# A graph attention with 8192 nodes: who clears the gather buffer, and behind which block each attention stands

## The reference

```python
feats   = (x @ W).reshape(N, H, D)
a_self  = einsum('nhd,hd->nh', feats, att_self)
a_neigh = einsum('nhd,hd->nh', feats, att_neigh)
scores  = leaky_relu(a_self.T[:, :, None] + a_neigh.T[:, None, :], 0.2)
scores  = scores - 1e10 * (1 - adj)
out     = einsum('hij,jhd->ihd', softmax(scores), feats) + bias
y       = layernorm(x + relu(out))
```

## Time and profile before

| | us |
|---|---|
| median of 3 runs (lowest, highest) | 844.21 (843.2, 846.03) |
| the profiled execution, its own time | 844.56 |
| its span, first to last instruction | 842.7 |
| TensorE busy with matmuls (share) | 600.1 (71%) |
| VectorE busy | 587.8 (70%) |
| GpSimd busy | 502.0 (60%) |
| ScalarE busy | 78.2 (9%) |
| moved by transfers | 291.79 MB |

### The profile page before, as it was taken

How to read it: one execution, slowest core, us unless ns; L and a number is a source line. 1 busy time by engine, 2 the same in 40 slices (tenths; PEclk the granted TensorE clock), 3 DMA queues, 4 the chain that set the end, 5 groups by cost and what they waited for, 6 DMA issues and landing times.

```text
span 842.7 us, 8722 instructions
## 1 busy us (share of the span) xinstructions
PE 600.1 (71%) x2132; PEld 289.6 (34%) x2133; DVE 587.8 (70%) x1683; ACT 78.2 (9%) x355; POOL 502.0 (60%) x464
## 2 busy tenths in 40 slices
PE   2766665588669797868888786976769685835564
PEld 1621111146314352433424251533335141504343
DVE  5567994641796878676666675677668977847885
ACT  1200000210010101000001000011020110102010
POOL 4100977777607777777777777766464757636400
PEclk9885555558979988886868695989799696958787
DMA  7999999999999999999999999999999999931100
GB/s 284 363 413 389 408 391 345 329 359 398 399 419 404 398 399 397 401 396 399 398 399 399 398 398 398 397 400 396 373 369 408 399 406 397 403 136 27 37 1 25
DMA packets 76230, 291.79 MB, mean 346 GB/s; under 512 B 31318, under 2 KB 39307, under 8 KB 43408
## 3 DMA queue, kind: packets, MB, share of 16 engines
q1 hardware_dynamic: 56784, 275.44, 83.4%
q0 software_dynamic: 14208, 10.46, 4.3%
q10 hardware_dynamic: 5184, 5.31, 1.9%
HBM read 294.39 MB, written 4.75 MB: 355 GB/s over the span
## 4 chain that ended last, share of the span: by engine, by line
DMA 52%; PE 27%; DVE 13%; issue 5%; SPq 1%; ACT 1%; DVEq 0%; ACTq 0%
DMA adj_sb<-in_adj_dram 51%; PE xt_ps L676 13%; PE codes L648 11%; DVE spare L926 2%; DVE head_mask L792 1%; PE ft_ps L633 1%; PE xt_ps L678 1%; PE ft_ps L717 1%; SPq L402 1%; DVE top L912 1%; DMA base<-in_L_gnn_att_self_dram 1%; DVE z L903 1%; DVE z L911 1%; DVE z L915 0%; DVE z L906 0%
## 5 line engine op out<-in xcount | busy, mean ns | idle before, releaser
L444 POOL DMA_INDIRECT near<-node_table,idx x444 | 489.6, 1103 | 278.6 <-issue 192.9
L648 PE MATMUL codes<-adj_sb,weights 128*128 128x512 bf16 x1024 | 349.5, 482 | 165.1 <-DMA adj_sb<-in_adj_dram 164.8
L648 PEld LDWEIGHTS codes<-adj_sb,weights 128*128 128x128 bf16 x1024 | 100.6, 109 | 393.7 <-issue 339.2
L676 PE MATMUL xt_ps<-spare,ident 128*128 128x360 f32 (+4 forms) x734 | 195.4, 416 | 29.6 <-DVE spare L926 29.6
L676 PEld LDWEIGHTS xt_ps<-spare,ident 128*128 128x128 f32 x734 | 135.5, 198 | 81.5 <-issue 41.8
L816 DVE MAX8 val<-codes 128x8 f32<-128x128 f32 x192 | 42.7, 284 | 140.7 <-PE codes L648 134.0
L926 DVE TENSOR_TENSOR spare<-near,spare 128x704 f32<-128x704 f32 (+12 forms) x64 | 101.1, 1641 | 9.1 <-ACT spare L571 9.1
L821 DVE MAX8 val<-codes 128x8 f32<-128x64 f32 (+2 forms) x156 | 19.6, 198 | 42.8 <-PE codes L648 42.0
L571 ACT ACTIVATE spare<-z 128x736 f32<-128x736 f32 (+10 forms) x16 | 14.9, 933 | 215.4 <-DVEq L918 215.4
L641 PE MATMUL codes<-place,weights 128*128 128x512 bf16 x64 | 31.3, 490 | 0.0
L872 DVE MAX8 key<-left 128x8 f32<-128x168 f32 (+2 forms) x79 | 28.7, 363 | 2.7
(11 more groups left out here) (156 smaller groups left out, 483.6 us busy)
## 6 DMA issues: line engine op xcount, KB each, us to landing
adj_sb<-in_adj_dram SPq DMA_DIRECT2D x256, 1024.0 KB, 16.7
near<-node_table,idx POOLq DMA_INDIRECT x444, 5.8
node_table<-spare ACTq DMA_DIRECT2D x4, 648.0 KB, 7.9
spare<-in_x_dram SPq DMA_DIRECT2D x4, 512.0 KB, 7.7
self_sb<-node_table ACTq DMA_DIRECT2D x16, 121.5 KB, 7.6
x_sb<-in_x_dram SPq DMA_DIRECT2D x4, 384.0 KB, 18.1
out_dram<-x_sb SPq DMA_DIRECT2D x1, 768.0 KB, 12.6
self_sb<-node_table ACTq DMA_DIRECT2D x16, 40.5 KB, 10.1
```

What stands on the lines that cost most here:

```text
L444: pool.indirect_dma_start(out=near[:, near_at(t) + k, :], out_offset=None, in_=table[:, :], in_offset=bass.IndirectOffsetOnAxis(ap=idx[t % ...
L648: last = pe.matmul(codes[i][:, :], weights[:, kk, :], adj_bf[q][:, k * GC:(k + 1) * GC, 1], start=False, stop=(kk == BITS - 1))
L676: last = pe.matmul(to[:, a:b, :], ident[:, :], slot_rows(t, s, a, b), start=(s == 0), stop=(s == W - 1))
```

## The change

Two edits. First, the clearing of `near` goes from POOL, where it stood behind `weights_ready`, to VectorE, as its first instruction; POOL still waits for it (`near_zeroed`) ahead of its first gather. Second, `ATTEND` is changed from turn 6 on: the turns 6 to 10 come three blocks apart, then after a space of four again three. With it the sums and finishes move. Behind the last packing stand two attentions (turns 14 and 15, at 64 and 67), and the sums of turns 13 to 15; turn 12's sums stand in block 62. Turns 6, 10 and 11 now stand behind the last block of a turn (39, 51 and 55), where before it was turn 8 (47).

```diff
-    ATTEND = [16, 20, 24, 28, 32, 36, 40, 44, 47, 50, 53, 57, 60, 64, 67, 70]
+    ATTEND = [16, 20, 24, 28, 32, 36, 39, 42, 45, 48, 51, 55, 58, 61, 64, 67]
...
-            pool.wait_ge(weights_ready, 1)
-            pool.memset(near[:, :, :], 0.0).then_inc(near_zeroed, 1)
 
             pool.wait_ge(table_written, 16 * XG)
             pool.wait_ge(near_zeroed, 1)
...
+            dve.memset(near[:, :, :], 0.0).then_inc(near_zeroed, 1)
             dve.wait_ge(params_loaded, 64)
 
             step(dve.memset(wa, 0.0))
```

## The result

The changed kernel takes 830.39 us (median of 4 runs, 829.19 to 831.54) against 844.8 us for the kernel before (median of 4, run beside it): a ratio of 0.9834, 95% interval 0.9812 to 0.9856. The forecast was 832.0, in a range of 826 to 842. The profiled execution took 829.19, with a span of 827.4 us against 842.7, so 15.3 us less. The text takes that span apart first, since the sum hit the total with terms that were partly wrong.

The account below looks back on a forecast made before the run. Adjacency transfers were taken to bound the kernel between about 45 and 746 us, the rest lying at the ends. From 844.56 us, -2.0 (head), +1.5 (body) and -11.7 (tail) gave 832.4, or 832.0 against the median; range 826 to 842.

Parts of the forecast that it names:

- the sum: Whole kernel: 844.56 us profiled, with -2.0 (head), +1.5 (body) and -11.7 (tail), gives 832.4; 832.0 against the median.
- The tail: Behind the last packing: last scores start at 793.5 instead of 805.26, held by the last turn's gather; 11.7 us gained.
- The path into the last two blocks: Blocks 61 and 62: finish 11 and attention 13 fit there, weighing 13 ending at 748.4, last packing staying at 748.3.
- The delay of 1.4 us: Tail: a microsecond or two allowed on the tight path, so turn 15's sort ends at 759.4, not 758.0.
- The head: Kernel's start: memset on VectorE makes the first feature copy about 6 us earlier; 2.0 us gained, bounds 0 and 3.5.
- The step that SyncE frees quarter 7: Head: x_r's issue and the bias occupy SyncE until 30.93, so quarter 7 is issued at most 3.1 us earlier.
- the step beneath: Head, 32 to 44 us: transfers at 335 GB/s against 427 leave 1.1 MB missing, or 2.6 us.
- the port: Head: whether VectorE's memset holds up POOL's patterns; some 1 us of the 6 lost, or nothing by the skill.
- The body: Turns 6 to 15, moved one to three blocks earlier: 1.5 us lost to likelier followers, bounds 0 and 8.
- a follower: Body: a further late weighing, made likelier by four turns in a row at three blocks.
- The price of 3.2 us: Body: loss per sort standing between attention and weighing, from turn 8's window at 294 GB/s instead of some 400.
- the slower rival: Blocks 39 to 62: VectorE becomes the bound, each late weighing costing 3.2 us; 846.9 us in all, chance 0.09.

Follow-up runs that it names:

- the two reordered kernels: Weighing put between peeling and sorting: for turn 6 in the changed kernel, 828.88 us; for turn 8 in the kernel before, 844.31 us.

## Why the prediction came out right, step by step

**The tail (forecast 11.7 within 8.7 to 15.5, measured 15.0 to the last scores).** The mechanism was the one forecast, and the runs with the gather cut and with the list alone show it: the end hangs on the last turn's gather, not on the 20.7 us of work moved. The size was too small. From the end of the last packing to the last scores the sum had 793.5 - 748.3 = 45.2 us, and it is 790.30 - 748.98 = 41.3. Of these 3.9 us the sort is 1.2 (it ends 9.9 us behind the last packing, where I had put 11.1), the gather's length -0.7 (20 issues took 29.1 us, not 28.4), and the landing 3.4. That last term is the mis-sized one: I let the rows arrive 5.8 us behind the start of the last issue, from the median in the earlier trace rows, but ScalarE's word ended VectorE's wait at 790.22, 2.4 us behind the last start at 787.79. The gather's two terms are not steady from trace to trace: in six of the eight with this order the 20 issues take 27.9 us, and the word comes 2.4 to 3.8 us behind the last start (3.8 in the second trace of the changed kernel). Together they are 2.6 to 4.0 us less than the sum had, here 2.7. The landings of the changed kernel show why, by the time of issue: first from 400 to 480 us, beside the matrix, then from 746 to 752, where its last quarter lands.

```profile
DMA to landing us min/median/max: 5.5/5.7/6.7
...
DMA to landing us min/median/max: 2.1/2.5/3.9
```

So the 5.8 was taken from gathers beside the stream (the landings behind it are all of issues before 714 us) and used for one that runs when the stream is over.

**The path into the last two blocks** was walked rightly: weighing 13 ends at 746.7, the last packing at 748.98, and nothing but 0.2 us of waiting stands between the last codes and the sort. The delay of 1.4 us that I had put in for caution did not come. The path has little slack, and that it held is shown by these rows alone.

**The head (forecast -2.0, measured nothing).** The step that SyncE frees quarter 7 at most 3.1 us earlier was right in its direction: it came to 0.4, and 1.7 in the second trace. Two sizes were off: the memset ended at 12.35 and not near 10.0, since it started late, so the first feature copy gained 3.7 us instead of 6; and x_r's issue grew by 1.5 us. But the step beneath, that 1.1 MB missing in the ring is 2.6 us to be had, failed. With the hold taken away, neither quarter 16 nor the last one moves by more than traces of one order differ. It is the same step as with the dips: bytes missing in a stretch were counted as time lost.

On the port: POOL's two index patterns beside the memset take 0.26 and 0.19 us at 3.49 and 3.71, and end when they ended before (3.9 us). So there is no contention to be seen, as the Trainium skill says of such an instruction (SBUF — State Buffer, "Who interferes with whom"). For the gather, the Trainium skill's inference in that section, that tensor_tensor does not stop the writing of descriptors, does not carry over: the three issues beside VectorE's weighing at 774.69 take 1.70, 2.23 and 1.62 us, not 1.00, and in the kernel before one takes 8.42 us beside a tensor_tensor:

```profile
95.93 8.42 POOL L444 DMA_INDIRECT near<-node_table,idx  x1 [0.30 <-issue]
...
94.79 8.69 DVE L972 TENSOR_TENSOR spare<-spare,z 128x8192 f32<-128x8192 f32 x1
```

Such an issue also reads its indices from SBUF. No run separates that read from the writing of descriptors, so the rows show that the issue is held, and not which part of it.

**The body (forecast +1.5, measured +0.6 at the last packing, head included, which is within the spread).** That one late weighing goes and one comes, at block 42, was right, and so was a follower. The price of 3.2 us for each was wrong, as the two reordered kernels show. That the sum came out near the measured time is in this part luck: two wrong terms (-2.0 and +1.5) nearly cancelled. By that same finding the slower rival was mispriced: TensorE waited 6.0 and 5.1 us in the changed kernel, and the stream ended as before.

## What to carry to other kernels

When work is moved off the end of a kernel, ask which transfer now ends last, and count from the moment that allows it to start; here 20.7 us moved gave 15, and the rest became a wait of 5.3 us for rows. And take a transfer's time to land from a stretch with the same traffic. In a part that is paced by transfers, a dip of the rate on the page is not yet lost time: look whether the landings behind it come later, and test it by an edit that only removes the dip. Here the share of the DMA engines told the two kinds apart: it fell in the dips that cost nothing and stayed full in the one that cost 6.6 us. What gained time there was less work of the transfers themselves.

## What the runs showed of the hardware

8192 reads of 4 bytes, 0.03 MB in all, cost the stream 6.6 us at its end, with the DMA engines' share at 1.00 and 325 GB/s instead of 399. Indirect gathers issued beside the stream (400 to 480 us) landed 5.5 to 6.7 us behind their issue, those issued where it ended 2.1 to 3.9. A memset of 11,016 elements on VectorE takes 9.24 us, 0.84 ns per element, like POOL's 9.28, but began 2.3 us after VectorE had finished a small one. An issue on SyncE can hold the queue for 15 to 21 us (x_r, in both places that were tried on SyncE), where POOL issued the same transfer in 0.56 us.
